# One output-projection tile placed behind two tiles of transposes, and LayerNorm sums taken on ScalarE, in a fused attention and recurrent-layer kernel on eight cores

## The reference

```python
x = x + layernorm(attention(layernorm(x), Wq, Wk, Wv, Wo, bo))
x = x + layernorm(ffn(layernorm(x), wf, uf, ..., wo, uo, bo, in_c))
```

## Time and profile before

| | us |
|---|---|
| median of two runs | 3540.43 (3535.18 and 3545.67) |
| the profiled execution, slowest core | 3527.22 |
| its span, first to last instruction (core 6) | 3525.6 |
| spans of the eight cores | 3503.1 to 3525.6 |

### The profile page before, as it was taken

One profiled execution on the slowest core, in us unless ns is written; L12 is line 12 of the kernel. 1 busy time (PEld: TensorE's weight loads), 2 busy tenths in 40 slices (PEclk: granted clock), 3 DMA queues, 4 the chain that ended last, 5 costly groups with the idle time before them and its releaser, 6 DMA issues.

```text
span 3525.6 us, 31785 instructions; the slowest of 8 cores (3503.1 to 3525.6 us)
## 1 busy us (share of the span) xinstructions
PE 1938.1 (55%) x9395; PEld 927.4 (26%) x9540; DVE 1053.3 (30%) x1786; ACT 518.3 (15%) x1193; POOL 333.7 (9%) x510
## 2 busy tenths in 40 slices
PE   1666455554455554544542011899999996888000
PEld 0323222232232222322221011344444442333000
DVE  0434333343343433423332044221221221222222
ACT  1011111111111111112011033111111111111000
POOL 1010101101101011010111100000000001110111
PEclk9766566666665666656656555899999998999555
DMA  7010211111212111121111944100000003111333
GB/s 117 25 47 23 57 42 47 43 39 44 54 37 57 45 45 53 39 57 44 40 45 60 161 131 137 31 1 13 12 13 13 13 13 57 31 30 33 126 124 125
DMA packets 167405, 186.98 MB, mean 53 GB/s; under 512 B 109886, under 2 KB 122174, under 8 KB 167230
## 3 DMA queue, kind: packets, MB, share of 16 engines
q0 software_dynamic: 53456, 151.38, 16.4%
q1 hardware_dynamic: 113792, 33.57, 3.9%
HBM read 151.68 MB, written 58.72 MB: 60 GB/s over the span
## 4 chain that ended last, share of the span: by engine, by line
PE 52%; DVE 17%; issue 9%; DMA 9%; ACT 6%; another core or an unknown queue 4%; DVEq 2%; POOL 1%; ACTq 0%; POOLq 0%; SPq 0%
PE ps_p L1610 11%; PE ps_a L2054 10%; PE ps_a L2060 10%; PE ps_p L1474 5%; DMA xin<-x 4%; PE ps_p L2147 3%; PE ps_p L2154 3%; DVE otn L1776 3%; PE ps_a L1727 2%; DVE kst L1679 2%; DVE qst L1679 2%; DMA vst<-v_scr 2%; PE ps_rl L1760 2%; ACT pt_sb L1739 2%
## 5 line engine op out<-in xcount | busy, mean ns | idle before, releaser
L1739 ACT ACTIVATE pt_sb<-ps_a 128x512 bf16<-128x512 f32 x128 | 76.1, 594 | 1021.6 <-PE ps_a L1727 1021.6
L1760 PE MATMUL ps_ot<-pt_sb,vst 128*65 128x128 bf16 x256 | 63.0, 279 | 288.6 <-DMA vst<-v_scr 242.3
L2074 ACT ACTIVATE gat<-ps_a,biases 128x512 f32<-128x512 f32 x192 | 131.9, 687 | 584.8 <-PE ps_a L2060 584.8
L2084 DVE TENSOR_TENSOR cT<-cT,gat 128x512 f32<-128x512 f32 x64 | 44.3, 693 | 580.2 <-ACT gat L2074 580.2
L1610 PE MATMUL ps_p<-wq_sb,xlnT_t 128*128 128x512 bf16 x481 | 175.3, 540 | 44.3 <-DVE xlnT_t L1596 43.0
L1474 PE MATMUL ps_p<-wo_sb,zlT_t 128*128 128x512 bf16 x482 | 162.5, 510 | 59.7 <-DVE zlT_t L1460 59.2
L2054 PE MATMUL ps_a<-xtT_sl,wq_sb 128*128 128x512 bf16 x500 | 132.6, 409 | 51.3 <-DMA xtT_sl<-xt_scr 39.1
L2147 PE MATMUL ps_p<-qst,gat 128*128 128x512 bf16 x495 | 120.1, 383 | 60.2 <-DMA gat<-xt_scr 31.5
L1711 POOL DMA_DIRECT2D vst<-v_scr x128 | 96.0, 755 | 534.5 <-DMA v_scr<-vtok 469.5
L2060 PE MATMUL ps_a<-zb,wk_sb 128*128 128x512 bf16 x500 | 125.0, 391 | 0.6
L2154 PE MATMUL ps_p<-kst,zb 128*128 128x512 bf16 x508 | 120.6, 379 | 0.3
(11 more groups left out here) (165 smaller groups left out, 2756.9 us busy)
## 6 DMA issues: line engine op xcount, KB each, us to landing
xin<-x POOLq DMA_DIRECT2D x96, 512.0 KB, 4.7
xin<-xr POOLq DMA_DIRECT2D x32, 512.0 KB, 4.3
x<-x1t POOLq DMA_DIRECT2D x32, 512.0 KB, 3.0
out<-x1t POOLq DMA_DIRECT2D x32, 512.0 KB, 3.0
v_scr<-vtok SPq DMA_DIRECT2D x32, 256.0 KB, 2.0
vst<-v_scr POOLq DMA_DIRECT2D x128, 64.0 KB, 3.0
od<-orow SPq DMA_DIRECT2D x128, 64.0 KB, 1.8
zin<-od POOLq DMA_DIRECT2D x128, 64.0 KB, 2.9
```

The source lines that it names most:

```text
L1739: ch_exp.inc(sc.activation(pt_sb[:, gbuf * 512:(gbuf + 1) * 512], ps_a[:, abank * 512:(abank + 1) * 512], AF.Exp, scale=0.125))
L1760: inst = t.matmul(psot[0:65, pk4 * 128:(pk4 + 1) * 128], vst[:, vslot * 260 + pk4 * 65: vslot * 260 + (pk4 + 1) * 65], pt_sb[:, gbuf * 512 ...
L2074: ch_gev.inc(sc.activation(gat[:, gi * 512:(gi + 1) * 512], ps_a[:, pg * 512:(pg + 1) * 512], func, bias=biases[:, bcol + mt:bcol + mt + 1]))
```

## The change

There are two edits.

The first moves the output-projection tile `emit_P2(n - 1, 3, ...)`. It was called right after group 15; it is now called after the transposes of tiles 0 and 1 of the next batch and ahead of `emit_P1_front(n + 1, 2)`. This holds for n = 1 to 6. For n = 7 there is no next batch and the call stays where it was in the order; for n = 0 there is no such tile.

The second replaces `ln_stats_hy` by `ln_stats_sc` in the LayerNorm stage: the sum over the tile is no longer taken by DVE's `reduce_sum`, but by a second ACT pass (Copy with a running sum), and the function `ln_stats_hy` is deleted.

```diff
-            if grp % 4 == 3 and n >= 1:
+            if grp % 4 == 3 and grp < 15 and n >= 1:
                 emit_P2(n - 1, grp // 4, ODS_hist[n - 1])
...
         if n + 1 < B:
             emit_P1_qtr(n + 1, 0)
             emit_P1_qtr(n + 1, 1)
+            if n >= 1:
+                emit_P2(n - 1, 3, ODS_hist[n - 1])
             emit_P1_front(n + 1, 2)
             emit_P1_qtr(n + 1, 2)
             emit_P1_front(n + 1, 3)
             emit_P1_qtr(n + 1, 3)
             stk_vsp[n + 1] = (ch_stk.n, (ch_vsp[0].n, ch_vsp[1].n))
+        elif n >= 1:
+            emit_P2(n - 1, 3, ODS_hist[n - 1])
...
-        ln_stats_hy(P, ch_sum, ch_rst, xi, fjunk2, sl, s1, s2, mean,
+        ln_stats_sc(P, ch_rst, xi, sqj[:], fjunk2, sl, s1, s2, mean,
                     msq, rstd, D, wait=(chx, chx.n))
```

More of the change, by code:

```diff
@@ L89, in f_stat @@
         sc.activation(sq_junk2, xi, AF.Copy, accum_out=s1[:, sl])
[L90 to L118, removed]
         sc.drain()
```

## The result

The changed kernel is slower by 0.8%: the ratio of its times to those of the kernel before is 1.0076, with a 95% interval of 1.0059 to 1.0093, that is +27 us on 3543. The medians are 3575.5 us (43 executions) and 3543.2 us (42 executions). They include executions with a lower granted clock on one die, which the ratio leaves out, and so lie a little further apart than 27 us.

The account below looks back on a forecast made before the run. PE bounds the scan; elsewhere no engine is full, and a chain hopping between engines through in-order queues sets the time. Moved projection tile +61, sum on ACT -37, together +24 us on 3536: 3560 us, range 3537 to 3589.

Parts of the forecast that it names:

- The copies start where line 1460 stood: Six batch boundaries: DVE's eight copies start at 490.09, right behind group 15, and take 11.36 us.
- The chain from line 1460 to the residual keeps its 11.98 us: Boundary: from DVE's copy of the projection tile's transposes to its residual add, 11.98 us as before.
- Issue to Square pass, statistics, apply: Boundary: residual to load issue 2.34 us, then 6.39, 3.25 and 0.45 to tile 2's apply, 10.92 later than before.
- Nothing else changes behind the apply: Boundary: behind tile 2's apply the same work follows as before, only later; the whole move costs 61 us.
- The LayerNorm stage: Second block: with the sum on ACT, two tiles take 9.29 us instead of 11.53; first to last apply 143, gain 37.
- L: Landing time of an input load in the LayerNorm stage, taken as 4.1 us; two tiles take 5.19 us plus it.
- (a): Boundary rival: the load stays hidden, the move costs nothing; -37 us alone, 3499; chance 0.05.
- (b): Boundary rival: PE's 7.27 us wait goes at six boundaries, nothing replaces it; -81 us, 3455; chance 0.03.
- (c): LayerNorm rival: loads bind; landing 5.4 us gives sum +43 (3579), 6.3 gives +57 (3593); chance 0.11.
- (d): LayerNorm rival: landing past 6.6 us makes the second edit a loss; from 7.25 total 71 us slower; chance 0.05.
- The base: Whole kernel's time before the change, taken as 3536 us, the mean of the three executions shown.

Follow-up runs that it names:

- changed kernel with the load ahead: Changed kernel, but GpSimd issues the load of tile 2 ahead of the moved projection tile's store; 0.9919 of the kernel before.
- kernel before with the load ahead: Kernel before, only GpSimd's queue reordered so the load of tile 2 goes out ahead of the store; 1.0002 of the kernel before.
- second half moved: Kernel before with sum on ACT, only projection tile's statistics, residual, store moved behind tile 0's transposes, load of tile 2 ahead of store; 0.9868.

## Why the prediction was right

It said 3560 us with a range of 3537 to 3589, and +24 us as the sum of +61 and -37. Measured are 3575.5 and a ratio worth +27. By its steps:

- *The copies start where line 1460 stood.* Right: line 1650 begins 1.20 us after the last reciprocal, line 1460 before 1.19. The eight take 11.37 us, forecast 11.36.
- *The chain from line 1460 to the residual keeps its 11.98 us.* Wrong by 0.8: it is 515.93 - 503.15 = 12.78, and over the six boundaries 12.91 in the mean against 12.04 before. Nearly all of this is in PE's sixteen matmuls. The first bias add begins 4.73 us after the copy in both kernels, but the second waits 1.98 us for PE, where it had waited 1.18. The reason is in the clock, below.
- *Issue to Square pass, statistics, apply.* 2.34, 6.14, 3.25 and 0.38 against 2.34, 6.39, 3.25 and 0.45. Together the apply is 11.42 us later, measured from group 15, forecast 10.92; in the mean of the six it is 11.0, forecast 10.2.
- *Nothing else changes behind the apply.* Wrong by another 0.4 us a boundary (89.51 - 78.05 = 11.5 to the next group, where 11.0 of it were there at the apply). The part as a whole is 6 x 11.5 = 69 us on the cores of the two profiles and 63 in the mean of all eight; the timed run of the first edit alone says 70 with an interval of some 23 us on each side. The forecast of 61 lies a little under the two figures of the traces and inside the interval.
- *The LayerNorm stage.* Right: L is 3.9 in the median, forecast 4.1; first to last apply 140 to 143 us, forecast 143. The detail that the applies would stay in pairs, 3.4 and 5.9 apart, holds only in part: the distances are 3.35, 5.55, 3.62, 5.03, 4.16 and 4.55 us at first, go on in turn short and long (3.72 and 5.60 in the tenth and eleventh), and are 4.48 and 4.41 at the end. With the second edit alone the pairs stay to the end (3.35, 6.07 and 3.35 us last). The loop of two tiles has the same length either way. That two loads close together delay the second, which evens them out, is only argued.
- *The rivals.* (a) needed a load that goes out before the store, (b) a chain of tile 2 that does not start at it; the row of 517.72 shows the store ahead, after 41.05 us at the head of the queue. (c) and (d) needed landings of 5.4 us and more; the median is 3.9.
- *The base.* 3536 as the mean of three executions was 7 us under the median of 42. That is the largest part of the 15.5 us between 3560 and 3575.5; 3 are the sum (+27 for +24), the other 5 lie between the medians and the ratio.

**The term that was missing.** TensorE's clock at the start of the `Wo` matmuls and at the start of the wq matmuls of tile 2, first boundary (stretch; length; busy us of PE, PEld, DVE, ACT, POOL; PEclk, DMA share, GB/s), before and after:

```profile
491.50:497.00 5.50, 5.48 (x24) 2.29 (x24) 1.00 (x2) 0.00 (x0) 0.00 (x0) 0.69 0.00 0
518.50:523.50 5.00, 4.95 (x15) 1.96 (x15) 0.69 (x1) 0.00 (x0) 0.00 (x0) 0.63 0.00 0
```

```profile
504.20:509.70 5.50, 5.50 (x14) 1.98 (x15) 0.69 (x1) 0.00 (x0) 0.00 (x0) 0.51 0.01 3
531.20:536.20 5.00, 4.93 (x12) 1.75 (x13) 0.69 (x1) 0.01 (x1) 0.00 (x0) 0.50 0.00 0
```

A window of 5.5 us from the start of the `Wo` matmuls has a granted clock of 0.69 before, 0.51 after, and 5.0 us from the start of the wq matmuls 0.63 and 0.50. In both kernels the `Wo` matmuls start at the low level (1.2 GHz) and the engine goes over to the high one (2.4 GHz) in the course of them: before the change the clock is 0.50 up to 494.5, 3.0 us after their start, and 0.93 in the 2.5 us behind it; after the change it is 0.50 up to 509.5, 5.3 us after their start, and 0.97 in the 1.0 us behind it. The granted clock ahead of them is 0.50 in both. What PE did there differs: attention groups ahead of the `Wo` matmuls in the one, eight groups of transposes in the other, and 18.76 us of idling ahead of tile 2 instead of 3.11 us. The second bias add comes 7.4 to 7.7 us after the copy at all six boundaries after the change, 6.5 to 6.9 before. The other traces repeat it: with the eight groups of transposes ahead (first edit alone, and changed kernel with the load ahead) it is 7.1 to 7.6 at all twelve, with attention groups ahead (second edit alone, kernel before with the load ahead, second half moved) 6.2 to 6.7 at 17 of 18, and 7.6 at one. So the delay goes with the order, though not at that one boundary. For the wq matmuls of tile 2 the same distance (copy of the transposed tile to the second copy-out) is 7.2 to 7.4 us at the first three boundaries and 6.2 to 6.3 at the last three, against 6.3 to 6.7 before: there it goes either way. I had taken the lengths of before as they were; about 0.9 us of each boundary is this term, 5 of the 63 to 69 us. No experiment was made on the clock alone, so why the clock rises later is open.

## What to carry to other kernels

In an in-order queue, a store that waits for a late result delays every load behind it; before moving a block of work, list what each of its DMA issues stands in front of, since the load that the old order hid under other work may be uncovered by the new one. Filling a wait is worth it only if the work that fills it was not itself the cover of something: here waits of 7.27 and 3.11 us were traded for one of 18.76. Where a chain hops between engines, let the statistics of the next tile depend on nothing but its own load, and then look for the buffer loop that binds next. And a wait that goes need not be gained in full: of 174 us of waits for v, about half came back here as waits for ACT.

## What the runs showed of the hardware that was not expected

**The final stage differs in length, by pairs of cores.** The code of the final stage (loads and stores of 512 KB, line 2190 after) is the same in all kernels. In the profile after it takes 274, 276, 262, 260, 276, 277, 250 and 251 us on cores 0 to 7. Landing time of its loads on core 5 and on core 7 of that execution:

```profile
DMA to landing us min/median/max: 4.2/5.5/5.9
```

```profile
DMA to landing us min/median/max: 4.5/4.7/4.8
```

Two neighbours (0 and 1, 2 and 3, 4 and 5, 6 and 7) have about the same length (within 4 us) in the traces read. In the profile of the second edit alone it is cores 2 to 5 that take 274 to 279 us and the other four 250; in that of before, cores 6 and 7 take 257 and 256, the rest 249 to 251. So it seems to depend on the execution and not on the kernel, whose code is the same there. The profile after has its slowest core in a long pair, that of before in one of 256: of the 51 us between the two profiled executions, 20 come from here (core 5: 276.7, core 6 of before: 256.6), and 31 are there at the start of the stage. In the long pairs the loads land 0.8 us later, which over 31 periods is the 25 us of the stage. That two neighbouring cores share what slows them is only suggested by the pairs; what it is, and why only in some executions, stays open.

**The landing time of one and the same load goes with its company.** 512 KB from GpSimd's queue landed in 3.9 us in the median in the LayerNorm stage with loads and 256 KB stores in turn, in 4.7 or 5.5 in the final stage with 512 KB stores, and in 6.3 to 7.0 where two loads and a store were issued together. The Trainium skill, "DMA: Bandwidth & Descriptors", section "Anatomy of one DMA", fits it with 3.2 us (2.0 plus the bytes over 436 GB/s); no load of that stage landed in less than 3.4 us, on any core before or after, so the trace does not agree with it for these loads (the stores of 512 KB, 3.0 us in the median before and 3.1 to 3.4 after, lie close to it). Had the LayerNorm stage been estimated by it, the gain would have been put at 51 us instead of the 38 that were measured.
